# A selective scan whose inputs come back from memory: VectorE's product reads delta B in PSUM

## The chip, the cores and the metric

The kernel runs on one core of a Trainium2 chip. The core has five engines that follow their own queues and meet at semaphores: TensorE (PE in the profile), VectorE (DVE), ScalarE (ACT), GpSimd (POOL), and SyncE (SP), which here only issues DMAs. The metric is the device time of one execution in microseconds (us). Lower is better.

## The reference, cut to what matters

The program is two transformer-like layers over 4 batches of 1024 tokens with 128 channels. The first layer is attention and a mixture of experts; the second is a Mamba-style selective scan and a second mixture of experts. Only the scan is touched by the change:

```python
proj = x_conv @ W_xproj                 # u = x_conv, 128 channels
B_sel, C_sel = proj[..., :16], proj[..., 16:32]
delta = softplus(proj[..., -1])         # one number a token
deltaA = exp(delta[..., None, None] * A)              # A: 128 channels x 16 states
deltaB_u = delta[..., None, None] * B_sel[:, :, None, :] * u[..., None]
def step(h, inp):
    a_t, bu_t, c_t = inp
    h = a_t * h + bu_t                  # 128 x 16 recurrences
    y_t = einsum('bdn,bn->bd', h, c_t)
    return h, y_t
...
y = y + x_conv * D_param
y = y * silu(z)
return y @ W_out
```

Each batch has 128 x 16 = 2048 independent recurrences of 1024 steps.

## The kernel before

The scan stage is one block, `selective_scan`. A tile has 128 partitions (rows) and the 1024 tokens of a batch along the free side. A **group** is 8 channels x 16 states = 128 rows, so a batch has 16 groups and the stage 64. For each group:

- ScalarE makes `da`, the exponential of delta times A (L2098), up to `AHEAD` = 3 groups ahead, into five buffers.
- TensorE makes the group's rows of delta times u, by multiplying with a 0/1 matrix `sel` that copies each of 8 channels to 16 rows. To keep float32 it does this twice, for a rounded part `du_hi` and for the remainder `du_lo` (L1938, L1939: 2 halves of 512 tokens, so 4 matmuls a group). The result lies in one of two PSUM tiles, `ps_x`. Before it writes one, TensorE waits for the scan two groups back.
- VectorE multiplies `ps_x` in place by `brep`, the 16 states' B repeated over the rows (L1995), and runs the recurrence over the tokens as one instruction (L2000), which writes `st`. The scan waits for the product (same engine, by a semaphore), for `da`, and for a free `st` buffer.
- GpSimd multiplies `st` by `crep` into `hc` (L2110).
- Every fourth group TensorE sums `hc` over the states into `ps_y` (L1949).

The order of all this is one list, `scan_plan()`. Every engine walks the same list and does its part of each step, in order, so a step that waits holds everything behind it on its engine. Between the groups of batch b stand the steps that prepare batch b+1: normalisation and transpose (`norm`, `turn`, L2045, L1907, L2049), a causal convolution by four shifted matmuls (`conv`, L1900) and its activation (`u`, L2056), the gate (`z`), the row for delta (`raw`, `soft`, L2069 to L2078), delta itself on VectorE (`delta`, L1976, behind group 9), B and C repeated over the rows (`rep`, TensorE L1919, ScalarE L2089), and `du` and `du_lo`. For the first batch VectorE makes `du` and `du_lo` (L1980, L1983); for the other three GpSimd does (L2116, L2122). In every batch ScalarE makes `du_hi` between them (L2084). Between the groups of batch b also stand the last steps of batch b-1: `y` (L2011), `out` (L1926, L2017) and `stats` (L156, L160). `turn`, `conv`, `z`, `raw`, `rep` and `out` share two PSUM banks, `ps_w`, in turn.

SyncE's whole part in this block is two loads of `sel`, 512 KB each, at its start. VectorE converts them (L1986, L1988).

The two lines that VectorE runs 64 times each are

```python
e.wait_ge(x_pe.sem, x_pe.at[key])                    # TensorE has filled ps_x[i]
e.tensor_tensor(ps_x[i][:, :], ps_x[i][:, :], brep[k][:, :], ALU.mult)        # L1995
...
e.tensor_tensor_scan(st[n % NST_BUF], da[n % NDA], ps_x[i], 0.0, ALU.mult, ALU.add)   # L2000
```

## Time and profile before

| | |
|---|---|
| median of 3 runs | 1983.67 us (1980.42 to 1984.81) |
| the profiled execution | 1981.38 us, of which the recorded span is 1979.6 us |
| the scan's block in the span | from 1370 us to 1661 us, 15% |
| busy over the whole span | PE 82%, POOL 65%, DVE 61%, ACT 39% |
| busy between 1394 and 1646 us | DVE 235.9 of 252 us, POOL 180.2, PE 176.8, ACT 139.2 |
| first and last scan (L2000) | start at 1396.3 and at 1644.9 us |

Read the busy shares stage by stage. The page's shares of the whole span say that TensorE is the busiest engine, and in attention it is. In the scan's block VectorE is, at 94%. The table of stretches, the groups of instructions by line, and the order of instructions in time are the views that show this stage. In a row of the timeline, the number in brackets is the idle time of that engine just before, with what ended it.

### The profile page before, as it was taken

How to read it: one execution, taken by the hardware profiler on the slowest of the kernel's cores; microseconds unless marked ns; L12 is line 12 of the kernel's file. 1: busy time of each engine (PE TensorE's matmuls, PEld its weight loads, DVE VectorE, ACT ScalarE, POOL GpSimd, SP SyncE). 2: the span in 40 equal slices, each digit the busy share in tenths (PEclk: the TensorE clock that was granted, in tenths of full speed). 3: DMA queues.
4: the chain of work that ended last, by engine and by line, in shares of the span. 5: the costliest groups of instructions: out<-in, count | busy, mean ns of one | idle time of the engine just before them, and what ended most of it. 6: DMA issues, size and time to landing. Idle time of an engine off the chain costs nothing. (4 is left out here: it accounts for less than half of the span.)

```text
span 1979.6 us, 26522 instructions
## 1 busy us (share of the span) xinstructions
PE 1617.7 (82%) x9024; PEld 1115.1 (56%) x9024; DVE 1201.4 (61%) x2409; ACT 764.4 (39%) x1278; POOL 1288.5 (65%) x1091
## 2 busy tenths in 40 slices
PE   5799999999999999999999899998776765347670
PEld 3455656665567556676565787886333333236560
DVE  6876666667665666756661456664799997511124
ACT  2245444354443544434445333222866530102120
POOL 4588898789887898878888511100477775481516
PEclk7799999999999999999999999999988876577885
DMA  6223122112211222121210200000000002022213
GB/s 168 65 76 96 44 65 65 37 40 65 54 44 44 65 47 51 41 68 40 58 33 12 62 1 1 1 1 22 0 1 0 0 0 88 29 71 66 79 50 83
DMA packets 82740, 90.67 MB, mean 46 GB/s; under 512 B 12448, under 2 KB 52276, under 8 KB 82608
## 3 DMA queue, kind: packets, MB, share of 16 engines
q1 hardware_dynamic: 78512, 80.97, 16.6%
q0 software_dynamic: 4096, 8.02, 1.4%
q8 instruction: 73, 1.20, 0.3%
q14 instruction: 59, 0.48, 0.1%
HBM read 24.05 MB, written 14.68 MB: 20 GB/s over the span
## 5 line engine op out<-in xcount | busy, mean ns | idle before, releaser
L835 DVE CUSTOM_DVE_ANT_0 ring<-ring,mask 128x128 f32<-128x128 f32 (+7 forms) x512 | 383.8, 769 | 184.3 <-PE ring L697 183.8
L921 ACT ACTIVATE prob<-ring 128x512 f32<-128x512 f32 x576 | 315.2, 597 | 297.0 <-PE ring L712 293.2
L975 POOL TENSOR_TENSOR acc<-acc,prob 128x512 f32<-128x512 f32 x272 | 353.6, 1300 | 72.6 <-ACT prob L921 48.8
L728 PE MATMUL ps_o<-prob,v 128*64 128x256 f32 x2304 | 281.5, 386 | 4.2 <-issue 3.8
L697 PE MATMUL ring<-k,x 128*128 128x512 f32 (+3 forms) x768 | 249.6, 405 | 37.3 <-ACT prob L921 22.3
L711 PE MATMUL ring<-x,k 128*128 128x512 f32 x576 | 257.2, 447 | 25.0 <-DVE neg_m L835 15.7
L712 PE MATMUL ring<-x,k 128*128 128x512 f32 x576 | 229.1, 398 | 0.0
L697 PEld LDWEIGHTS ring<-k,x 128*128 128x128 f32 x768 | 136.4, 197 | 145.1 <-ACT prob L921 51.2
L728 PEld LDWEIGHTS ps_o<-prob,v 128*64 128x64 f32 x2304 | 154.0, 136 | 106.1 <-issue 38.4
L972 POOL TENSOR_TENSOR acc<-prob 128x512 f32<-128x512 f32 x144 | 184.1, 1279 | 7.9 <-ACT prob L921 6.6
L942 POOL TENSOR_TENSOR other<-other,sin 128x512 f32<-128x512 f32 x96 | 136.5, 1422 | 58.1 <-DVE other L814 57.6
L711 PEld LDWEIGHTS ring<-x,k 128*128 128x128 f32 x576 | 109.1, 189 | 99.8 <-issue 43.6
L2000 DVE TENSOR_TENSOR_SCAN m_st<-m_da,m_ps_x 128x1024 f32<-128x1024 f32 x64 | 146.4, 2287 | 2.2
L2310 POOL DMA_INDIRECT c_got<-slots_out,d_slot x64 | 66.1, 1032 | 110.9 <-DMA slots_out<-wo 92.0
L944 POOL TENSOR_TENSOR rot<-rot,other 128x512 f32<-128x512 f32 x96 | 129.7, 1351 | 7.5
L1666 POOL TENSOR_TENSOR first_h<-first_h,e_scaled 128x512 f32<-128x512 f32 x8 | 10.2, 1276 | 175.3 <-DVE e_scaled L1548 175.3
L712 PEld LDWEIGHTS ring<-x,k 128*128 128x128 f32 x576 | 109.6, 190 | 19.6 <-issue 6.9
L2110 POOL TENSOR_TENSOR attn_t<-m_st,m_crep 128x1024 f32<-128x1024 f32 x32 | 78.7, 2459 | 62.1 <-DVE m_st L2000 62.1
L827 DVE TENSOR_TENSOR rot<-rot,other 128x512 fp32r<-128x512 f32 x64 | 72.3, 1130 | 69.6 <-ACT other L903 69.6
L1534 DVE TENSOR_TENSOR e_both<-e_silu,ps_moe 128x512 f32<-128x512 f32 x88 | 60.4, 687 | 87.5 <-PE ps_moe L1378 69.0
L2234 DVE CAST c_xt_hi<-c_tr 128x512 fp32r<-128x512 f32 x16 | 11.1, 692 | 166.0 <-PE c_tr L2189 116.4
L2213 PE MATMUL c_dn<-w,c_hid 128*128 128x128 f32 x512 | 70.3, 292 | 49.9 <-issue 48.8
(302 smaller groups left out, 3179.8 us busy)
## 6 DMA issues: line engine op xcount, KB each, us to landing
x<-other SPq DMA_DIRECT2D x256, 128.0 KB, 2.4
x<-rot SPq DMA_DIRECT2D x128, 128.0 KB, 2.4
slots_in<-zeros SPq DMA_DIRECT2D x2, 2048.0 KB, 8.7
slots_out<-wo SPq DMA_DIRECT2D x16, 256.0 KB
gate<-slots_in SPq DMA_DIRECT2D x11, 256.0 KB
e_w<-in_w SPq DMA_DIRECT2D x3, 704.0 KB, 6.7
x<-shift SPq DMA_DIRECT2D x128, 2.0 KB
first_h<-in_x SPq DMA_DIRECT2D x4, 512.0 KB, 4.9
```

The source lines that it names most:

```text
L697: mm = e.matmul(ps[:, c0:c1], x1[g % 2][:, h, qs], k1[g % 3][:, c0:c1], start=True, stop=True)
L711: e.matmul(banks(step, BANK), k1[g % 3][:, ks], x1[g % 2][:, :, qs], start=True, stop=False)
L712: e.matmul(banks(step, BANK), k2[g % 3][:, ks], x2[g % 2][:, :, qs], start=False, stop=True).then_inc(s2_pe.sem, 1)
L728: mm = e.matmul(ps_o[s * D:(s + 1) * D, qb % 2 * 2 * P:(qb % 2 + 1) * 2 * P], v[g % 2][:, kb, :], prob[i % NPROB][:, s * 2 * P:(s + 1) * 2 ...
L835: e.tensor_tensor_reduce(ps, ps, mask_1[:, SEQ - n:SEQ], 1.0, -3.0 * NEG, ALU.add, ALU.min, neg_m[g % 2][:, c, h, qb % QPC:qb % QPC + 1]). ...
L921: e.activation(prob[i % NPROB][:, :], banks(("s2",) + key, BANK), ACT.Exp, scale=-1.0).then_inc(s2_exp.sem, 1)
L942: e.tensor_tensor(other[i][:, :], other[i][:, :], sin[:, cc], ALU.mult).then_inc(rotated.sem, 1)
L944: e.tensor_tensor(rot[i][:, :], rot[i][:, :], other[i][:, :], ALU.add).then_inc(rotated.sem, 1)
L972: e.tensor_tensor(total[:, :], first[:, :], tile[:, :], ALU.add).then_inc(summed.sem, 1)
L975: e.tensor_tensor(total[:, :], total[:, :], tile[:, :], ALU.add).then_inc(summed.sem, 1)
L2000: e.tensor_tensor_scan(st[n % NST_BUF][:, :], da[n % NDA][:, :], ps_x[i][:, :], 0.0, ALU.mult, ALU.add).then_inc(scan_dve.sem, 1)
L2110: e.tensor_tensor(hc[(b * NG + g) % NHC][:, :], st[r][:, :], crep[b % 2][:, :], ALU.mult).then_inc(hc_pool.sem, 1)
```

## The change

What the change does, in the order of the data:

- The repeated u comes by DMA. When ScalarE has made half of u (512 tokens), SyncE writes it to a new tensor in memory, `u_mem`. For each group SyncE then reads the group's 8 rows back, 16 times over, into a 128-row tile `x_rep`. There are `NX` = 5 such buffers with a semaphore each. The read waits for both halves of u, and for the product five groups back (it has read the buffer).
- TensorE's 256 matmuls by `sel` are gone, with `sel` and its two loads, `du`, `du_hi`, `du_lo`, and the PSUM tiles `ps_x`.
- delta times B is made once a batch and lies in a PSUM tile `ps_b`. For the first batch VectorE makes it (`delta_b`). For the others GpSimd multiplies `brep` by delta in place, and ScalarE copies the result to `ps_b` in a new step `b_in`, which waits for GpSimd and for the last product of the batch before. `brep` now has one buffer where it had two.
- VectorE's product reads `x_rep` in SBUF and `ps_b` in PSUM and writes a PSUM tile `ps_bu`. There is one `ps_bu`, so each product waits for the scan just before it. The first product of a batch also waits for `ps_b`.
- The rows of a tile are ordered by state and then channel (before: by channel and then state). That changes only the layout of `log_a`, `fold`, `w_b` and `w_c`.

```diff
-        steps += [[("rep", b, 0, 0)], [("rep", b, 0, 1), ("delta", b)], [("rep", b, 1, 0), ("du", b)], [("rep", b, 1, 1), ("du_lo", b)]]
+        steps += [[("rep", b, 0, 0)], [("rep", b, 0, 1), ("delta", b)], [("rep", b, 1, 0), ("delta_b", b)], [("rep", b, 1, 1)]]
...
             plan += ahead[g]
+            if g == NG - 1 and b + 1 < BATCH:
+                plan.append(("b_in", b + 1))
...
-                    for c in range(NC2):
-                        cc = slice(c * BANK, (c + 1) * BANK)
-                        e.matmul(ps_x[i][:, cc], sel[:, of * P:(of + 1) * P], du_hi[k][:, cc], start=True, stop=False)
-                        mm = e.matmul(ps_x[i][:, cc], sel[:, of * P:(of + 1) * P], du_lo[k][:, cc], start=False, stop=True)
-                    mm.then_inc(x_pe.sem, 1)
...
                 elif kind == "group":
                     b, g = key
-                    k, i, n = b % 2, (b * NG + g) % 2, b * NG + g
-                    e.wait_ge(x_pe.sem, x_pe.at[key])
+                    n = b * NG + g
+                    e.wait_ge(x_in[n % NX], (n // NX + 1) * 16)
                     if g == 0:
+                        e.wait_ge(*b_ready(b))
                         e.wait_ge(act.sem, act.at["rep", b, 1, NC2 - 1])
-                    e.tensor_tensor(ps_x[i][:, :], ps_x[i][:, :], brep[k][:, :], ALU.mult).then_inc(bu_dve.sem, 1)
+                    if n:
+                        e.wait_ge(scan_dve.sem, scan_dve.at[behind(b, g, 1)])
+                    e.tensor_tensor(ps_bu[:, :], x_rep[n % NX][:, :], ps_b[:, :], ALU.mult).then_inc(bu_dve.sem, 1)
...
-                    e.wait_ge(*du_made("du", b))
-                    if b >= 2:
-                        e.wait_ge(x_pe.sem, x_pe.at[b - 2, NG - 1])
-                    e.activation(du_hi[b % 2][:, :], du[:, :], ACT.Copy).then_inc(act.sem, 1)
+                    e.wait_ge(delta_b_pool.sem, delta_b_pool.at["delta_b", b])
+                    e.wait_ge(bu_dve.sem, bu_dve.at[b - 1, NG - 1])
+                    e.activation(ps_b[:, :], brep[:, :], ACT.Copy).then_inc(act.sem, 1)
...
         def sync(e):
-            e.dma_start(sel_in[:, :], a["sel"][:, 0:half]).then_inc(sel_in0, 16)
-            e.dma_start(y[:, :], a["sel"][:, half:2 * half]).then_inc(sel_in1, 16)
+            for step in plan:
+                kind, key = step[0], step[1:]
+                if kind == "u":
+                    b, c = key
+                    cc = slice(c * BANK, (c + 1) * BANK)
+                    e.wait_ge(act.sem, act.at[step])
+                    e.dma_start(u_mem[b, :, cc], u[b % 2][:, cc]).then_inc(u_out, 16)
+                elif kind == "group":
+
+                    at = key[0] * NG + key[1]
+                    for n in range(at + NX - 1 if at else 0, min(at + NX, BATCH * NG)):
+                        b, g = divmod(n, NG)
+                        rows = slice(group_at(g) * FG, (group_at(g) + 1) * FG)
+                        e.wait_ge(u_out, (b + 1) * NC2 * 16)
+                        if n >= NX:
+                            e.wait_ge(bu_dve.sem, bu_dve.at[behind(b, g, NX)])
+                        e.dma_start(x_rep[n % NX][:, :], u_mem[b, rows, :].rearrange("(o c) t -> o c t", o=1).to_broadcast([NST, FG, SEQ])).then_inc(x_in[n % NX], 16)
```

ScalarE's queue at the start of the scan, from the raw row of delta (`m_raw`) to the first exponentials (`m_da`), before:

```order
L2069 ACTIVATE m_raw<-m_ps_w 128x512 x2
L2074 ACTIVATE m_soft<-m_raw 128x1024
L2078 ACTIVATE m_soft<-m_soft 128x1024
L2089 ACTIVATE m_brep<-m_ps_w 128x512 x2
L2084 ACTIVATE m_du_hi<-m_du 128x1024
L2089 ACTIVATE m_crep<-m_ps_w 128x512 x2
L2098 ACTIVATE m_da<-m_delta,m_a_neg 128x1024 x4
```

and of the changed kernel:

```order
L2054 ACTIVATE m_raw<-m_ps_w 128x512 x2
L2059 ACTIVATE m_soft<-m_raw 128x1024
L2063 ACTIVATE m_soft<-m_soft 128x1024
L2075 ACTIVATE m_brep<-m_ps_w 128x512 x2
L2075 ACTIVATE m_crep<-m_ps_w 128x512 x2
L2084 ACTIVATE m_da<-m_delta,m_a_neg 128x1024 x4
```

The rounding of du, which waited for VectorE, no longer stands between B's rows and C's.

ScalarE's queue where batch 0 ends and batch 1 begins (`m_z` is the gate of batch 0, the three `m_da` behind it are for groups 16 to 18), before:

```order
L2062 ACT_TABLE_LOAD
L2062 ACTIVATE m_z<-m_ps_w 128x512 x2
L2064 ACT_TABLE_LOAD
L2098 ACTIVATE m_da<-m_delta,m_a_neg 128x1024 x3
L2045 ACTIVATE m_xn<-first_h,m_nmr,m_rstd 128x128 x4
```

and of the changed kernel:

```order
L2047 ACTIVATE m_z<-m_ps_w 128x512 x2
L2049 ACT_TABLE_LOAD
L2084 ACTIVATE m_da<-m_delta,m_a_neg 128x1024 x2
L2068 ACTIVATE m_ps_b<-m_brep 128x1024
L2084 ACTIVATE m_da<-m_delta,m_a_neg 128x1024
L2030 ACTIVATE m_xn<-first_h,m_nmr,m_rstd 128x128 x4
```

The copy of delta B to PSUM is put in after the exponential for group 18, and before that for group 19.

SyncE's queue from the start of the block, where before there were the two loads of `sel`, now reads:

```order
L2122 DMA u_mem<-m_u 128x512 x2
L2132 DMA m_x_rep<-u_mem 128x1x1024 x8
L2122 DMA u_mem<-m_u 128x512
L2132 DMA m_x_rep<-u_mem 128x1x1024 x2
L2122 DMA u_mem<-m_u 128x512
L2132 DMA m_x_rep<-u_mem 128x1x1024 x14
```

The two writes of the next batch's u stand among the reads for this batch's groups: the first between the reads for groups 7 and 8, the second between those for 9 and 10.

## Rows read from the trace of the kernel before

**Rows 1.** By stretch: us; busy PE, PEld, DVE, ACT, POOL; clock; DMA share; GB/s.

```profile
1394.00:1460.00 66.00, 45.95 (x165) 23.22 (x166) 56.67 (x34) 48.03 (x58) 41.28 (x18) 0.85 0.00 1
1580.00:1646.00 66.00, 38.03 (x149) 18.55 (x147) 65.13 (x56) 14.98 (x13) 46.73 (x22) 0.76 0.00 0
```

**Rows 2.** DVE groups by line, 1365 to 1652 us: busy, mean ns | idle before, releasers.

```profile
L2000 DVE TENSOR_TENSOR_SCAN m_st<-m_da,m_ps_x 128x1024 f32<-128x1024 f32 x64 | 146.4, 2287 | 2.2
L1995 DVE TENSOR_TENSOR m_ps_x<-m_ps_x,m_brep 128x1024 f32<-128x1024 f32 x64 | 77.6, 1213 | 14.0 <-PE m_ps_x L1939 13.8
```

**Rows 3.** DVE in order of time at the scan's start.

```profile
1388.91 1.23 DVE L1976 SCALAR_TENSOR_TENSOR m_delta<-m_raw,m_soft 128x1024 f32<-128x1024 f32 x1 [12.21 <-ACT m_soft L2078]
1390.17 1.23 DVE L1980 TENSOR_TENSOR m_du<-m_delta,m_u 128x1024 f32<-128x1024 f32 x1
...
1395.08 1.23 DVE L1995 TENSOR_TENSOR m_ps_x<-m_ps_x,m_brep 128x1024 f32<-128x1024 f32 x1 [1.34 <-PE m_ps_x L1939]
1396.34 2.29 DVE L2000 TENSOR_TENSOR_SCAN m_st<-m_da,m_ps_x 128x1024 f32<-128x1024 f32 x1
1402.12 1.23 DVE L1995 TENSOR_TENSOR m_ps_x<-m_ps_x,m_brep 128x1024 f32<-128x1024 f32 x1 [3.49 <-PE m_ps_x L1939]
```

**Rows 4.** DVE in order of time, steady state, and a wait.

```profile
1443.19 2.29 DVE L2000 TENSOR_TENSOR_SCAN m_st<-m_da,m_ps_x 128x1024 f32<-128x1024 f32 x1
1445.40 1.21 DVE L1995 TENSOR_TENSOR m_ps_x<-m_ps_x,m_brep 128x1024 f32<-128x1024 f32 x1
1446.64 2.29 DVE L2000 TENSOR_TENSOR_SCAN m_st<-m_da,m_ps_x 128x1024 f32<-128x1024 f32 x1
1452.58 1.23 DVE L1995 TENSOR_TENSOR m_ps_x<-m_ps_x,m_brep 128x1024 f32<-128x1024 f32 x1 [3.66 <-PE m_ps_x L1939]
```

**Rows 5.** ACT in order of time at the scan's start.

```profile
1382.53 0.69 ACT L2056 ACTIVATE m_u<-m_ps_w,m_cb 128x512 f32<-128x512 f32 x1 [2.75 <-PE m_ps_w L1900]
...
1388.78 1.07 ACT L2089 ACTIVATE m_brep<-m_ps_w 128x512 f32<-128x512 f32 x2
```

**Rows 6.** PE in order of time at the scan's start: C's rows.

```profile
1389.41 1.98 PE L1919 MATMUL m_ps_w<-m_u,m_w_c 128*128 128x512 f32 x4 [2.25 <-ACT m_brep L2089]
```

**Rows 7.** ACT groups by line, 1365 to 1652 us.

```profile
L2089 ACT ACTIVATE m_crep<-m_ps_w 128x512 f32<-128x512 f32 x8 | 4.6, 584 | 0.3 <-PE m_ps_w L1919 0.2
L2084 ACT ACTIVATE m_du_hi<-m_du 128x1024 fp32r<-128x1024 f32 x4 | 4.2, 1057 | 23.0 <-POOL m_du L2116 21.4 <-DVE m_du L1980 1.6
```

**Rows 8.** DMA issues: KB each, median us to landing.

```profile
m_st<-in_sel SPq DMA_DIRECT2D x1, 512.0 KB, 3.8
wo<-in_sel SPq DMA_DIRECT2D x1, 512.0 KB, 5.2
first_h<-in_x SPq DMA_DIRECT2D x4, 512.0 KB, 4.9
first_h<-in_x SPq DMA_DIRECT2D x2, 256.0 KB, 3.2
```

**Rows 9.** PE groups by line, 1365 to 1652 us.

```profile
L1938 PE MATMUL m_ps_x<-m_du_hi,m_sel 128*128 128x512 f32 x128 | 68.2, 533 | 41.4 <-DVE m_st L2000 39.0 <-DVE m_du_lo L1983 2.5
L1939 PE MATMUL m_ps_x<-m_du_lo,m_sel 128*128 128x512 f32 x128 | 56.3, 440 | 0.0
```

**Rows 10.** PE alone by stretch: us, busy (instructions), clock, DMA.

```profile
1446.00:1449.00 3.00, 3.00 (x16) 0.50 0.02 5
```

**Rows 11.** PE in order of time: the state sums, and two taps of the convolution.

```profile
1415.07 1.92 PE L1949 MATMUL m_ps_y<-attn_t,m_fold 128*32 128x512 f32 x16 [1.20 <-POOL attn_t L2110]
1416.93 1.99 PE L1900 MATMUL m_ps_w<-attn_t,m_w_tap 128*128 128x512 f32 x4
...
1445.74 3.64 PE L1949 MATMUL m_ps_y<-attn_t,m_fold 128*32 128x512 f32 x16 [1.51 <-POOL attn_t L2110]
```

**Rows 12.** ACT and POOL in order of time: from a scan to the next batch's delta.

```profile
1412.64 2.38 POOL L2110 TENSOR_TENSOR attn_t<-m_st,m_crep 128x1024 f32<-128x1024 f32 x1 [1.07 <-DVE m_st L2000]
...
1418.95 0.69 ACT L2056 ACTIVATE m_u<-m_ps_w,m_cb 128x512 f32<-128x512 f32 x1 [3.59 <-PE m_ps_w L1900]
...
1430.15 1.06 ACT L2078 ACTIVATE m_soft<-m_soft 128x1024 f32<-128x1024 f32 x1
```

More of the change, by code:

```diff
@@ L1700 @@
 NDA, AHEAD, NST_BUF = 5, 3, 4
+NX, NW = 5, 2
 def group_at(i):
@@ L1723, in scan_plan @@
         plan += [("conv", 0, c, j) for j in reversed(range(TAPS))] + [("u", 0, c)]
-    plan += [("table", 0), ("raw", 0, 0), ("raw", 0, 1), ("soft", 0), ("sel",), ("rep", 0, 0, 0), ("rep", 0, 0, 1), ("delta", 0), ("du", 0),
-             ("du_lo", 0), ("rep", 0, 1, 0), ("rep", 0, 1, 1)]
+    plan += [("table", 0), ("raw", 0, 0), ("raw", 0, 1), ("soft", 0), ("rep", 0, 0, 0), ("rep", 0, 0, 1), ("delta", 0), ("delta_b", 0),
+             ("rep", 0, 1, 0), ("rep", 0, 1, 1)]
     pend = []
```

115 lines of the change are left out of this document (46 added, 69 removed).

## The prediction, made before the changed kernel ran

> **What bounds the kernel now.** The views were read in this order: the table of stretches, VectorE's groups by line, VectorE's instructions in order of time, then the engines that feed it. In the scan's block VectorE is busy 56.7 of 66 us in an early stretch and 65.1 of 66 in the last one, and no other engine comes near [rows 1]. Two lines carry it: 64 scans of 2.287 us and 64 products of 1.213 us, 224 us together [rows 2]. VectorE's idle time before a product sums to 14.0 us, of which 13.8 ended when TensorE had filled `ps_x` [rows 2]. The reader should see three numbers there: the scan and the product are at a fixed duration, the idle time is only 14 us, and all of it is TensorE's. So a change that relieves TensorE can win at most these 13.8 us and what it saves before the first scan. TensorE's own removed work, 68.2 + 56.3 us of matmuls [rows 9], is worth nothing by itself, because VectorE covers it.
>
> **VectorE's two steps themselves don't get shorter.** Before, the product reads one tile in PSUM (`ps_x`) and one in SBUF (`brep`) and writes PSUM. After, it reads `ps_b` in PSUM and `x_rep` in SBUF and writes PSUM. The scan reads `da` in SBUF and a PSUM tile in both. The places are the same in number and kind; only the product is no longer in place. An elementwise step of the same size on SBUF alone (delta, du) takes 1.23 us [rows 3], as the product does behind an idle time. So I take no change of duration. The bound on both sides is 0.02 us each, the difference between a product at 1.21 and one at 1.23 [rows 4]: 64 x 0.02 = 1.3 us.
>
> **The start of the scan: a gain of 3.0 us.** Before, delta starts at 1388.91 and the first product only at 1395.08, because du, its rounding on ScalarE, du_lo and four matmuls stand between [rows 3]. After, delta is followed by one product, `delta_b`, by the 0.03 us after which du follows delta now: 1388.91 + 1.26 + 1.23 = 1391.40. But the first group's product also waits for C's last rows. TensorE makes them from 1389.41 to 1391.39 [rows 6], and ScalarE's copy of the last half takes 0.58 [rows 7], so it ends at about 1392.0. Before, this was hidden behind du_hi. The product starts at 1392.05 and the scan 1.26 later (1395.08 to 1396.34, [rows 3]), at 1393.3. That is 3.0 us before 1396.34. The first exponential takes 1.14 us behind C's rows and ends in time.
>
> **Does the first read of u arrive by then?** u's second half is ready at 1382.53 + 0.69 = 1383.2 [rows 5]. No row shows the landing of a write to memory; the nearest is a 256 KB load, 3.2 us. A 512 KB load with 4 KB rows, as `x_rep` is, lands after 3.8 us [rows 8]. So 1383.2 + 3.2 + 3.8 plus 0.1 for the issue is 1390.3, before 1392.05. The margin is 1.7 us. If the write took 5 us the loss would be 0.1, so I take 0, with 0 to 2 us as the bounds.
>
> **The waits for TensorE: a gain of 12.5 us.** Of the 13.8 us, 1.3 lie before the first product and are counted above. The others (3.49 and 3.66 are the largest, [rows 3, 4]) go, if what replaces TensorE is in time. What is late next? `x_rep` is asked for when the product five groups back has ended, so four groups or some 14 us ahead. The two loads of `sel`, of the same size and shape, landed 3.8 and 5.2 us after issues 0.4 us apart [rows 8], so the second needed 1.8 us more. VectorE uses 512 KB in 3.6 us. `da` is made three groups ahead and loses a wait: ScalarE now idles 21.4 us for GpSimd's du [rows 7]. For `ps_b` ScalarE must copy 1024 columns between the last product of a batch and the next product. A copy of that size takes 1.06 us [rows 7], the scan above it 2.29: hidden, with some 1.1 us to spare. If ScalarE were late by its longest other step of the kind, 1.14 us, it would cost 3 x 0.1. Behind this wait stands only the exponential for group 19, needed three groups later. On SyncE the writes of u hold the reads behind them until ScalarE has made u; the reads for groups 8 and 10 then start some 4 us late, against a lead of 14.
>
> **The new wait for the scan: a loss of 5.5 us.** Now the product starts 2.21 us after the scan's start, and the scan takes 2.29: it starts 0.08 before the scan is recorded as ended [rows 4]. With a wait for an instruction of the same engine, the next starts 0.03 after the end (delta at 1388.91 takes 1.23, du starts at 1390.17) [rows 3]. A product that starts so is also the longer kind, and its scan follows after 1.26 instead of 1.24. A group thus goes from 2.21 + 1.24 = 3.45 to 2.29 + 0.03 + 1.26 = 3.58, or 0.135 us more. Of 63 places between two groups, 18 have other VectorE work between (delta, y, out, stats: 1, 6, 6 and 5 in the four batches), which covers the wait. Another 5 are those where VectorE already idled for TensorE right after a scan; they lose 0.03 each. The other 40 lose 0.135. Together 5.4 + 0.15 = 5.5 us. The bounds are 0 (it costs nothing) and 63 x 0.16 = 10.
>
> The Trainium skill speaks to this place: its page "VectorE: DVE Perf Modes", section "The DRAIN you can't avoid", says that the next instruction can't start before the pipe of the last is empty, and that a semaphore between two instructions costs nothing extra. By that rule the loss would be 0 and the time that of the first rival below. The row shows a start 0.08 us before the recorded end where nothing is waited for and 0.03 after it where something is, so I go by the row.
>
> **The sum.** 3.0 + 12.5 - 5.5 = 10.0 us. The profiled execution took 1981.38, of which the span is 1979.6; 10.0 less is 1971.4. It lies 2.3 below the median of the three runs, so in the terms of the median the forecast is 1983.67 - 10.0 = 1973.7 us. Behind the scan nothing changes: the last sums, y and out wait for GpSimd and run as before.
>
> **Rival 1, the wait is free.** The loss of 5.5 is 0 because the start 0.08 early is only overlap in the record. The time is 1983.7 - 15.5 = 1968.2. For it: the recorded end may lie behind the last read. Against it: the scan behind the product waits too, and starts 1.24 after a product of 1.21. Chance 0.12.
>
> **Rival 2, TensorE's clock drops and the preparation of the next batch becomes late.** From 1446 to 1449 us TensorE is busy throughout at a granted clock of 0.50, the lower of its levels (1.2 of 2.4 GHz) [rows 10]. There the state sums take 3.64 us instead of 1.92, behind an idle time of 1.51 [rows 11]. With 124 us of matmuls gone TensorE will idle more often, and more of the block may run so. The tightest chain in the first batch: a scan ends, GpSimd multiplies (1412.64 to 1415.02), TensorE sums (1.92) and does two taps (1.99), ScalarE makes u at 1418.95 and the last step of softplus at 1430.15 [rows 11, 12]. From the scan's end at 1412.6 that is 18.6 us, and at the lower clock 1.7 + 2.0 more, 22.3. VectorE asks for it six groups later, after 6 x 3.58 = 21.5 us. So it waits 0.8 us, and in the next two batches not at all, since out and stats stand between too. With as much again at `y` in each batch, up to 3 us. The time is 1976.7. Chance 0.14.
>
> **Rival 3, a longer product.** If reading one PSUM tile and writing another costs 0.1 us a product, 6.4 us of the 10 are lost, and at 0.16 all. The time is 1980 to 1986. For it speaks only that no row shows this form. Chance 0.10.
>
> **Rival 4, slower: the reads of u don't keep pace.** Each read fetches the same 8 rows 16 times, and no row shows such a read. VectorE will need 248.6 - 12.5 + 5.5 = 241.6 us from the first scan to the last, 3.83 a group on average. The mechanism decides from there: below 137 GB/s VectorE waits for memory at every group. If each read took the 4.9 us of a 512 KB load in the first stage [rows 8], one after another, 64 of them take 314 us, 69 more than 64 x 3.83. That is 1973.7 + 69 = 2043 us. Against it: the two loads of `sel` ran at 1.8 us each. Chance 0.08. That u isn't in the rows where it is needed, and the change doesn't do what it says, I rule out by the code.
>
> **How the numbers follow.** The forecast has 0.56. A measurement of this kernel can tell about 0.2% (4 us) from no change, so faster means below 1979.7. Forecast and rival 1 and most of rival 2 lie there: 0.56 + 0.12 + 0.12 = 0.80, and I take 0.79. Rival 3 and the rest of rival 2 are the same, 0.12. Slower is rival 4, 0.09 with the odd case. The range takes in rival 1 with 2 us for the spread of the runs (1966) and reaches through rival 2 and half of rival 3 (1983); rival 4 lies outside.
>
> **What would show it.** In the profile after: 64 products at 1.21 to 1.23 us, each starting 0.03 us after its scan's end, a group at 3.58 us; no idle time of VectorE before a product beyond 3 us in all; the first scan 3 us earlier after delta's start (4.4 us behind it where it is 7.4 now); reads of 512 KB landing in under 6 us; PEclk lower in the block. I am wrong if VectorE waits for `x_rep` at more than the first group, if the product's mean is above 1.25, if delta waits for softplus in more than one batch, or if the first product waits for `u_mem`.

## The result, and the profile after

| | before | after | ratio, 95% interval |
|---|---|---|---|
| first comparison, 13 runs each | 1983.42 us | 1978.71 us | 0.9978 [0.9970, 0.9987] |
| once more on another chip, 28 and 6 runs | 1933.61 us | 1927.39 us | 0.9966 [0.9954, 0.9978] |
| span of the profiled execution | 1979.6 us | 1975.8 us | |
| first and last scan | 1396.3 and 1644.9 | 1394.3 and 1639.2 | |

The change makes the kernel faster by 0.2 to 0.3%, some 4.4 to 6.6 us, where 10.0 were forecast. The time lies in the range that was given, but the size was wrong by about a factor of two. The second row is from a chip on which a later stage did less work (last section), so only its ratio is used.

VectorE's groups by line of the kernel after, 1365 to 1652 us, answer to [rows 2]:

```profile
L1985 DVE TENSOR_TENSOR_SCAN m_st<-m_da,m_ps_bu 128x1024 f32<-128x1024 f32 x64 | 146.3, 2286 | 2.2
L1980 DVE TENSOR_TENSOR m_ps_bu<-m_x_rep,m_ps_b 128x1024 f32<-128x1024 f32 x64 | 78.4, 1225 | 5.9 <-ACT m_crep L2075 0.8 <-DVE m_st L1985 0.5
```

The product's idle time has fallen from 14.0 to 5.9 us, and nothing in it is TensorE's any more. The scan is as long as it was, the product 12 ns longer. From this view the block should be some 8 us shorter. It is less, and the next one tells why. VectorE in order of time at the scan's start, the counterpart of [rows 3]:

```profile
1389.80 1.23 DVE L1966 SCALAR_TENSOR_TENSOR m_delta<-m_raw,m_soft 128x1024 f32<-128x1024 f32 x1 [15.09 <-ACT m_soft L2063]
1391.06 1.23 DVE L1970 TENSOR_TENSOR m_ps_b<-m_brep,m_delta 128x1024 f32<-128x1024 f32 x1
1393.06 1.23 DVE L1980 TENSOR_TENSOR m_ps_bu<-m_x_rep,m_ps_b 128x1024 f32<-128x1024 f32 x1 [0.76 <-ACT m_crep L2075]
1394.32 2.29 DVE L1985 TENSOR_TENSOR_SCAN m_st<-m_da,m_ps_bu 128x1024 f32<-128x1024 f32 x1
1396.71 1.23 DVE L1980 TENSOR_TENSOR m_ps_bu<-m_x_rep,m_ps_b 128x1024 f32<-128x1024 f32 x1
1397.98 2.29 DVE L1985 TENSOR_TENSOR_SCAN m_st<-m_da,m_ps_bu 128x1024 f32<-128x1024 f32 x1
```

The first scan starts 4.52 us after delta, where it was 7.43. The two scans here are 3.66 apart, and so are nearly all that have no other work between: of the 63 distances 45 are of this kind, 44 of them 3.65 to 3.68 long and one 4.01. In the kernel before, the plain distance is 3.445. Within a group, the product starts 2.39 after the scan's start (2.21 in [rows 4]) and the next scan 1.265 after the product's (1.24). Of this, idle time shows half, and without a name. The product's 5.9 us are 0.8 and 0.5 that the view puts down to somebody and 4.6 that it doesn't, which is 0.10 at each of these places (a scan of 2.29, the product 2.39 after its start). The other half can't show there: before, the product started 0.08 us ahead of the scan's recorded end, and the loss of such an overlap is no idle time. **Distances from scan to scan** are the view that shows all of it.

Stretches (us; busy PE, PEld, DVE, ACT, POOL; clock; DMA share; GB/s), beside [rows 1]:

```profile
1394.00:1460.00 66.00, 34.55 (x118) 12.12 (x119) 63.67 (x38) 51.31 (x64) 43.47 (x19) 0.77 0.66 164
1580.00:1646.00 66.00, 19.41 (x92) 6.38 (x96) 59.50 (x53) 12.70 (x12) 43.74 (x21) 0.58 0.36 88
```

VectorE is busy 63.7 us of the early stretch (56.7 before). TensorE lost a quarter and half of its work, and its granted clock fell from 0.85 to 0.77 and from 0.76 to 0.58. The DMA engines, idle before, move 164 GB/s. The transfers by issue (KB each, median us to landing) and ScalarE's copy of delta B:

```profile
m_x_rep<-u_mem SPq DMA_DIRECT2D x64, 512.0 KB, 4.6
u_mem<-m_u SPq DMA_DIRECT2D x8, 256.0 KB, 2.0
```

```profile
L2068 ACT ACTIVATE m_ps_b<-m_brep 128x1024 f32<-128x1024 f32 x3 | 3.1, 1021 | 7.6 <-DVE m_ps_bu L1980 7.6
```

The reads land in 4.6 us (median; 11.0 at most), against a lead of four groups, and no product waits for one.

**The ledger of the block.** From distances between scans: the groups in which VectorE waited for TensorE were 13.5 us longer than others of their kind, and all of that is gone. The 45 groups with nothing else between scan and product are 0.21 us longer each, 9.5 us, and the one at 4.01 another 0.35. (What holds that one isn't known. It is the 57th distance in the changed kernel, in its second run, with short reads, with more matmuls, and in the kernel before with the wait added, so neither the reads nor the new tiles make it.) That makes -13.5 + 9.5 + 0.35 = -3.65; the distance from first to last scan went from 248.55 to 244.85, -3.70. With the 2.9 us at the start, the block gives 6.6 us.

### The profile page after: what moved, and what is told of

Read it like the earlier page. It is cut to its first block and busy times, and to the rows that moved or that the text cites. A ratio compares the mean times of both kernels' runs of the same rounds, so it can differ in the third digit from the quotient of the medians.

```text
span 1975.8 us, 26070 instructions
## 1 busy us (share of the span) xinstructions
PE 1554.1 (79%) x8768; PEld 1067.1 (54%) x8768; DVE 1204.6 (61%) x2406; ACT 763.2 (39%) x1277; POOL 1277.5 (65%) x1088
## 5 line engine op out<-in xcount | busy, mean ns | idle before, releaser
L1985 DVE TENSOR_TENSOR_SCAN m_st<-m_da,m_ps_bu 128x1024 f32<-128x1024 f32 x64 | 146.3, 2286 | 2.2
L2096 POOL TENSOR_TENSOR attn_t<-m_st,m_crep 128x1024 f32<-128x1024 f32 x32 | 78.2, 2443 | 59.8 <-DVE m_st L1985 59.8
L960 POOL TENSOR_SCALAR_AFFINE_SELECT prob<-prob 128x512 f32<-128x512 f32 x128 | 91.2, 713 | 24.6 <-ACT prob L921 23.6
```

The costliest lines, as they stand in the source:

```text
L960: e.affine_select(tile[:, :], tile[:, :], [[0, G], [1, P]], ALU.is_ge, 0.0, base=0, channel_multiplier=-1).then_inc(causal.sem, 1)
L1985: e.tensor_tensor_scan(st[n % NST_BUF][:, :], da[n % NDA][:, :], ps_bu[:, :], 0.0, ALU.mult, ALU.add).then_inc(scan_dve.sem, 1)
```

## The experiments

Each kernel is compared with the kernel before, run beside it on the same chip. That took 1982.5 us beside the wait alone and the three kernels with operands elsewhere, 1932.6 beside short reads, more matmuls and the two spread versions of the changed kernel, and 1933.6 beside the rest. A plain group is the distance between two scans with only the product between them, in which no other engine is waited for.

| run | ratio, 95% interval | first to last scan | plain group |
|---|---|---|---|
| before | 1 | 248.6 us | 3.445 us |
| after | 0.9978 [0.9970, 0.9987] | 244.9 | 3.655 |
| after, again | 0.9966 [0.9954, 0.9978] | 244.8 | 3.655 |
| before, with the wait | 1.0042 [1.0025, 1.0059] | 255.3 | 3.66 |
| product in place in SBUF | 1.0258 [1.0241, 1.0275] | 302.6 | |
| delta B in SBUF | 1.0609 [1.0591, 1.0626] | 370.3 | |
| delta B in SBUF, two tiles | 1.0105 [1.0089, 1.0122] | 269.3 | |
| short reads | 0.9969 [0.9956, 0.9983] | 244.8 | 3.655 |
| more matmuls | 1.0046 [1.0030, 1.0062] | 255.9 | 3.655 |
| after, spread | 0.9935 [0.9919, 0.9951] | 238.6 | 3.655 |
| after, spread, C later | 0.9938 [0.9922, 0.9954] | 238.3 | 3.655 |
| before, spread | 0.9984 [0.9975, 0.9993] | 245.3 | 3.445 |
| after, two whole tiles | 0.9999 [0.9990, 1.0009] | 248.5 | 3.445 |
| after, three banks | 1.0001 [0.9992, 1.0011] | 252.5 | 3.505 |

### The wait alone, in the kernel before

```diff
                     e.wait_ge(x_pe.sem, x_pe.at[key])
+                    if n:
+                        e.wait_ge(scan_dve.sem, scan_dve.at[behind(b, g, 1)])
```

> The kernel before with one edit: each product also waits for the scan just before it. TensorE's matmuls, ps_x and everything else stay. My theory is that this wait is dearer than I predicted, 0.21 us a group (the product starts 0.10 us after the scan's recorded end, not 0.03) at the 40 places where nothing else covers it: the time should rise by 6 to 8.5 us, and the steady group go from 3.45 to 3.65 us. By the number of my prediction it rises by 5.5 us and the group is 3.58. The rival, that the missing gain lies in the new tiles or the reads from memory and the wait costs nothing, expects no change, within 1 us.

Measured: 1990.53 us against 1982.48, +8.0 us. VectorE in order of time, and the product's group:

```profile
1445.11 1.23 DVE L1997 TENSOR_TENSOR m_ps_x<-m_ps_x,m_brep 128x1024 f32<-128x1024 f32 x1
1446.37 2.29 DVE L2002 TENSOR_TENSOR_SCAN m_st<-m_da,m_ps_x 128x1024 f32<-128x1024 f32 x1
1448.76 1.23 DVE L1997 TENSOR_TENSOR m_ps_x<-m_ps_x,m_brep 128x1024 f32<-128x1024 f32 x1
1450.03 2.29 DVE L2002 TENSOR_TENSOR_SCAN m_st<-m_da,m_ps_x 128x1024 f32<-128x1024 f32 x1
```

```profile
L1997 DVE TENSOR_TENSOR m_ps_x<-m_ps_x,m_brep 128x1024 f32<-128x1024 f32 x64 | 78.6, 1229 | 16.7 <-PE m_ps_x L1939 12.2 <-DVE m_st L2002 0.5
```

The old kernel with one more wait has the new kernel's group: 2.39 from scan to product, 1.265 from product to scan. The two tiles, the place of delta B and the reads from memory have no part in it. First to last scan grows by 6.8 us in the trace, less than 45 times 0.21, since at a few places VectorE waited for TensorE anyway. The forecast had priced this wait at 5.5 us, the rival at 0. The time excludes the rival (+5.0 to +11.7 us by its interval); the forecast's size is excluded by the group's length, 3.66 and not 3.58.

### Why delta B lies in PSUM: two inputs in SBUF

Three kernels put the operands elsewhere. In the first there is no `ps_bu`: the product overwrites `x_rep`, and the scan reads `da` and `x_rep`, both in SBUF. The wait for the scan is gone (the next read into the buffer waits for the scan instead).

```diff
-                    if n:
-                        e.wait_ge(scan_dve.sem, scan_dve.at[behind(b, g, 1)])
-                    e.tensor_tensor(ps_bu[:, :], x_rep[n % NX][:, :], ps_b[:, :], ALU.mult).then_inc(bu_dve.sem, 1)
+                    e.tensor_tensor(x_rep[n % NX][:, :], x_rep[n % NX][:, :], ps_b[:, :], ALU.mult).then_inc(bu_dve.sem, 1)
...
-                    e.tensor_tensor_scan(st[n % NST_BUF][:, :], da[n % NDA][:, :], ps_bu[:, :], 0.0, ALU.mult, ALU.add).then_inc(scan_dve.sem, 1)
+                    e.tensor_tensor_scan(st[n % NST_BUF][:, :], da[n % NDA][:, :], x_rep[n % NX][:, :], 0.0, ALU.mult, ALU.add).then_inc(scan_dve.sem, 1)
```

> The changed kernel without ps_bu: the product writes back into its x_rep buffer in SBUF and the scan reads it there, so no product waits for a scan (the next read into a buffer waits for the scan instead). The wait theory expects a steady group of 3.45 us and a time 9 us below the changed kernel, near 1969.5 us or 14 us below before. The rival here: the scan now has two inputs in SBUF, beside GpSimd's steady multiplications; if that port is shared, scans or GpSimd's products get longer, by 0.2 us or more each, and the gain is gone.

Measured: 2033.21 us, +51, where the wait theory expected -14. Groups of VectorE and GpSimd:

```profile
L1983 DVE TENSOR_TENSOR_SCAN m_st<-m_da,m_x_rep 128x1024 f32<-128x1024 f32 x64 | 201.7, 3152 | 2.2
L1978 DVE TENSOR_TENSOR m_x_rep<-m_x_rep,m_ps_b 128x1024 f32<-128x1024 f32 x64 | 76.4, 1194 | 1.0 <-ACT m_crep L2073 0.8 <-issue 0.3
L2094 POOL TENSOR_TENSOR attn_t<-m_st,m_crep 128x1024 f32<-128x1024 f32 x32 | 101.6, 3181 | 62.6 <-DVE m_st L1983 62.6
```

The product with one input in SBUF and one in PSUM is fast (1194 ns), and the wait's price is saved. The scan with two inputs in SBUF takes 3152 ns for 2286, and GpSimd's product 3181 for 2443. In order of time the two engines are seen to take turns, the scan ending 2.15 us after GpSimd's step:

```profile
1427.93 2.35 POOL L2094 TENSOR_TENSOR m_hc<-m_st,m_crep 128x1024 f32<-128x1024 f32 x1 [2.23 <-DVE m_st L1983]
1429.00 3.43 DVE L1983 TENSOR_TENSOR_SCAN m_st<-m_da,m_x_rep 128x1024 f32<-128x1024 f32 x1
```

The second kernel leaves the scan as it is and gives the product two inputs in SBUF: delta B stays in two `brep` tiles, and ScalarE's copy goes away.

```diff
-        brep, crep = sb("brep"), [sb(f"crep{i}") for i in range(2)]
+        brep, crep = [sb(f"brep{i}") for i in range(2)], [sb(f"crep{i}") for i in range(2)]
...
-                    e.tensor_tensor(ps_bu[:, :], x_rep[n % NX][:, :], ps_b[:, :], ALU.mult).then_inc(bu_dve.sem, 1)
+                    e.tensor_tensor(ps_bu[:, :], x_rep[n % NX][:, :], brep[b % 2][:, :], ALU.mult).then_inc(bu_dve.sem, 1)
...
-                    e.activation(ps_b[:, :], brep[:, :], ACT.Copy).then_inc(act.sem, 1)
```

> The changed kernel with delta B left in SBUF in two buffers and no copy to PSUM: the product reads two tiles in SBUF and writes the one ps_bu, and waits for the scan as in the changed kernel. Only the place of one input changes. If the place of delta B doesn't matter, the time is the changed kernel's, within 1.5 us, and the product 1.23 us. If two inputs in SBUF beside GpSimd cost, product or GpSimd's step get longer; at 0.2 us a product that is 13 us slower.

Measured: 2102.38 us, +120, nine times the 13 that were named. GpSimd and VectorE in order of time:

```profile
1504.10 2.35 POOL L2089 TENSOR_TENSOR attn_t<-m_st,m_crep 128x1024 f32<-128x1024 f32 x1
1504.13 3.42 DVE L1978 TENSOR_TENSOR m_ps_bu<-m_x_rep,m_brep 128x1024 f32<-128x1024 f32 x1
1507.58 2.29 DVE L1983 TENSOR_TENSOR_SCAN m_st<-m_da,m_ps_bu 128x1024 f32<-128x1024 f32 x1
```

The end of a scan releases both engines at once. GpSimd's step starts 0.03 us earlier and takes its usual 2.35; the product takes 3.42 and ends 1.10 after it, about its own length of 1.2. So it did next to nothing while GpSimd worked. The third kernel uses the two banks (a bank is 512 columns of PSUM) that delta B left free for a second `ps_bu`, so that the product waits for the scan two back (against the changed kernel; the lines of the second kernel are in it too):

```diff
-                    if n:
-                        e.wait_ge(scan_dve.sem, scan_dve.at[behind(b, g, 1)])
-                    e.tensor_tensor(ps_bu[:, :], x_rep[n % NX][:, :], brep[b % 2][:, :], ALU.mult).then_inc(bu_dve.sem, 1)
+                    if n >= 2:
+                        e.wait_ge(scan_dve.sem, scan_dve.at[behind(b, g, 2)])
+                    e.tensor_tensor(ps_bus[n % 2][:, :], x_rep[n % NX][:, :], brep[b % 2][:, :], ALU.mult).then_inc(bu_dve.sem, 1)
...
```

> As the one with delta B in SBUF, and the PSUM room so won holds a second ps_bu: a product waits only for the scan two groups back. Against that kernel only the wait is removed. The wait theory expects a group of 3.45 us and 9 us less than that kernel. The prediction's size expects 5.5 us less; the rival that the wait costs nothing expects no difference.

Measured: 2002.17 us, 100 less than its neighbour and 20 more than the kernel before. Nine less than the neighbour had been expected, so this pair doesn't price the wait: taking it away also moved a clash with GpSimd off VectorE at most groups, as the rows show. Only the plain group, 3.445, is as the theory has it. In order of time:

```profile
1502.59 2.29 DVE L1984 TENSOR_TENSOR_SCAN m_st<-m_da,m_ps_bu 128x1024 f32<-128x1024 f32 x1
1504.79 1.21 DVE L1979 TENSOR_TENSOR m_ps_bu<-m_x_rep,m_brep 128x1024 f32<-128x1024 f32 x1
1504.95 3.23 POOL L2090 TENSOR_TENSOR attn_t<-m_st,m_crep 128x1024 f32<-128x1024 f32 x1 [3.49 <-DVE m_st L1984]
...
1508.15 2.34 POOL L2095 TENSOR_TENSOR m_brep<-m_brep,m_delta 128x1024 f32<-128x1024 f32 x1
1508.24 3.35 DVE L1979 TENSOR_TENSOR m_ps_bu<-m_x_rep,m_brep 128x1024 f32<-128x1024 f32 x1
```

Without the wait the product is 0.16 us ahead of GpSimd's step, and now GpSimd's is the one drawn out (3.23 for 2.35). Where GpSimd happened to be first (1508.15), the product pays again (3.35). Whoever starts first goes through, the other stands. The Trainium skill's page "SBUF — State Buffer", section "SBUF: two separate sides", states this as an exclusive lock between a VectorE instruction with two SBUF inputs and a GpSimd instruction that reads SBUF; all three traces agree, with the times above.

For the change this says what its odd placement is worth. Without delta B in PSUM there is a rival that is 20 or 120 us slower than the kernel before, not 5 us faster. But delta B takes two of the eight banks that the block uses, only one product tile is left, and that makes the wait.

### The reads of u, cut to almost nothing

```diff
+                        some = SEQ if n < NX else 16
-                        e.dma_start(x_rep[n % NX][:, :], u_mem[b, rows, :].rearrange("(o c) t -> o c t", o=1).to_broadcast([NST, FG, SEQ])).then_inc(x_in[n % NX], 16)
+                        e.dma_start(x_rep[n % NX][:, 0:some], u_mem[b, rows, 0:some].rearrange("(o c) t -> o c t", o=1).to_broadcast([NST, FG, some])).then_inc(x_in[n % NX], 16)
```

> The changed kernel, with one part left out: from the sixth group on, each read of the replicated channels brings 16 of the 1024 tokens, so the remaining tokens of the tile are those of an earlier group (the output is not the reference's). The number of transfers and all waits stay; the 32 MB that they moved fall to about 3. Theory (the reads are hidden): product 1225 ns, steady group 3.655 us, time within 2 us of the changed kernel's 1978.7, ratio to the kernel before 0.9978. Rival (the reads cost VectorE or the start of the later stages something): the product falls back to the 1213 ns of the kernel before, -0.8 us over 64, and the time to 1976 or less, ratio 0.996.

Measured: 0.9969 [0.9956, 0.9983], the ratio of the changed kernel (0.9966) within its interval, and the product's row is the same to the nanosecond:

```profile
L1980 DVE TENSOR_TENSOR m_ps_bu<-m_x_rep,m_ps_b 128x1024 f32<-128x1024 f32 x64 | 78.4, 1225 | 6.6 <-ACT m_crep L2075 1.4 <-DVE m_st L1985 0.5
```

First to last scan is 244.83 us with short reads and 244.83 with full ones. The 32 MB of reads cost VectorE nothing. The 12 ns by which the product grew are not memory's either: the kernel before with the wait has 1229.

### More matmuls, for TensorE's clock

```diff
+EXTRA = 2
...
+                    if plan.index(step) > plan.index(("group", 0, 0)):
+                        for _ in range(EXTRA):
+                            e.matmul(bank[:, :], w_in[:, HID:2 * HID], h_t[:, cols(0, 0)], start=True, stop=True)
```

> The changed kernel with two further matmuls of 128x512 on TensorE ahead of each matrix product of the preparation from the first group on, into the same bank, whose results are overwritten: some 90 of them at about 0.6 us give back the 55 to 60 us of TensorE's busy time that the change took from the scan block. Theory (the clock in the block is of no account to VectorE): granted clock of the stretch 1400 to 1650 up from 0.72 towards the 0.83 of before, steady group still 3.655, time within 2 us of 1978.7. Rival (the lower clock costs the stages behind the block 1.9 us, since from the last scatter into the experts' slots to the end of the span the changed kernel took 188.2 us and the kernel before 186.1): that stretch falls back to 186.1 us and the time to 1976.8.

Measured: 1.0046, 9 us slower than the kernel before and some 14 slower than the changed one. Both expectations of the time were wrong. As expected, the plain group stayed at 3.655 while the granted clock of the stretch rose from 0.72 to 0.83, so the group's length doesn't come from the clock. But the extra work made the preparation late. VectorE's steps with a wait ahead:

```profile
1429.38 2.30 DVE L1970 SCALAR_TENSOR_TENSOR m_delta<-m_raw,m_soft 128x1024 f32<-128x1024 f32 x1 [1.24 <-ACT m_soft L2067]
...
1456.31 1.23 DVE L1984 TENSOR_TENSOR m_ps_bu<-m_x_rep,m_ps_b 128x1024 f32<-128x1024 f32 x1 [2.89 <-ACT m_ps_b L2072]
...
1473.60 0.69 DVE L2006 TENSOR_TENSOR m_scaled<-m_ps_w,gate 128x512 f32<-128x512 f32 x1 [1.68 <-PE m_ps_w L1933]
...
1479.65 0.69 DVE L2006 TENSOR_TENSOR m_scaled<-m_ps_w,gate 128x512 f32<-128x512 f32 x1 [1.89 <-PE m_ps_w L1933]
```

As a test of what the clock does to the time it fails, since two things changed. It does show how near the preparation stands to VectorE: about 60 us more of TensorE's work, spread over a block where it has over 100 idle, lengthened the block by 11 us. The chain of rival 2 was real, but the clock alone was not enough to pull it.

### The small work spread over the waits

The statistics of four tiles, eight instructions in one place, become one `bn_stats` behind each of four scans and four `bn_aggr` behind a fifth; y's second half comes one group later. Nothing is added or left out.

```diff
+ONE_ROW, FOUR = (5, 6, 7, 8, 11, 12, 13, 14), (10, 15)
...
-            if b and g in (5, 6):
-                plan.append(("stats", b - 1, g - 5))
+            if b and g in ONE_ROW:
+                plan.append(("row", b - 1, *divmod(ONE_ROW.index(g), 4)))
+            if b and g in FOUR:
+                plan.append(("four", b - 1, FOUR.index(g)))
+            if b and g == 2:
+                plan.append(("y", b - 1, 1))
```

> The changed kernel with VectorE's small work spread out, nothing added: the statistics of four tokens' tiles, until now eight instructions in one place, become one instruction behind each of four scans and four behind a fifth, and the second half of y is taken one group later. So 44 of the 63 places between a scan and the product that waits for it hold other work, where 18 did. Theory (the wait costs only where nothing lies between: scan's start to product's start 2.39 us without, 2.20 us and the work itself with work between): 26 x 0.18 = -4.7 us, less some 0.5 us for instructions that no longer follow on each other: the last scan 4.2 us nearer to the first than the 244.85 of the changed kernel, time 1974.5, ratio 0.9956. Rival (the loss lies in the single tile and the product's reads, not in the wait): within 1 us of 1978.7.

Measured: 0.9935 [0.9919, 0.9951], 12.7 us faster than the kernel before; first to last scan 238.6, 6.3 less than after, where 4.2 were expected. VectorE in order of time:

```profile
1477.82 2.29 DVE L1992 TENSOR_TENSOR_SCAN m_st<-m_da,m_ps_bu 128x1024 f32<-128x1024 f32 x1
1480.03 0.27 DVE L2020 BATCH_NORM_STATS2 stats<-first_h 128x6 f32<-128x128 f32 x1
1480.21 1.23 DVE L1987 TENSOR_TENSOR m_ps_bu<-m_x_rep,m_ps_b 128x1024 f32<-128x1024 f32 x1
1481.48 2.29 DVE L1992 TENSOR_TENSOR_SCAN m_st<-m_da,m_ps_bu 128x1024 f32<-128x1024 f32 x1
```

The statistic starts 2.21 us after the scan's start, as the product did in [rows 4], and the product at 2.39, as if nothing stood between. The group is 3.66 with the statistic and 3.655 without. A piece of work of 0.19 us is free in the shadow of the wait, 24 times. The control is the same spreading in the kernel before, where no product waits for a scan:

> The kernel before with the same spreading of the statistics and of y's halves as in the spread version, and nothing else. Theory (the spreading pays only where a product waits for the scan ahead of it, because a statistic of 0.2 us then stands in time that was idle anyway): in the kernel before no product waits for a scan, each single statistic adds its 0.19 us to a group of 3.45, the distance from first to last scan stays at 248.5 us within 1, ratio 1.000. Rival (spreading saves for a reason of its own, such as the wait between statistics and aggregates): -6 us as in the changed kernel, ratio 0.997.

Measured: 0.9984 [0.9975, 0.9993], first to last scan 245.3, so 3.3 less where 0 was expected. The same place in this kernel:

```profile
1487.86 2.29 DVE L2007 TENSOR_TENSOR_SCAN m_st<-m_da,m_ps_x 128x1024 f32<-128x1024 f32 x1
1490.07 0.27 DVE L2035 BATCH_NORM_STATS2 stats<-first_h 128x6 f32<-128x128 f32 x1
1490.25 1.22 DVE L2002 TENSOR_TENSOR m_ps_x<-m_ps_x,m_brep 128x1024 f32<-128x1024 f32 x1
1491.50 2.29 DVE L2007 TENSOR_TENSOR_SCAN m_st<-m_da,m_ps_x 128x1024 f32<-128x1024 f32 x1
```

Here the group is 3.64 with a statistic and 3.445 without: the 0.19 us are paid. That is the core of the theory. But spreading has a gain of its own that I had not foreseen, and the distances divide it. Some 2.2 us lie where VectorE waits for TensorE: 5.47 and 4.73 us at two places became 4.57 and 4.58, and at 5.80 and 5.39 a statistic was added and the distances are 5.02 and 5.39. Another 1.1 us are the statistics themselves: in one place the eight instructions make a group 1.18 us longer, apart 4 x 0.19 + 0.27 = 1.03, and the last four `bn_aggr` now fall behind the last scan. Only this second part can be in the changed kernel too, which has no waits for TensorE. Without it, its gain is 6.3 - 1.1 = 5.2, and that is what the theory gives: 44 places with other work, where there were 18, are 26 more, at some 0.2 us each.

In a further version the rows of C come behind the first group's exponentials, and GpSimd's first step waits for them in the product's stead (the first line is VectorE's, the others GpSimd's):

```diff
-                        e.wait_ge(act.sem, act.at["rep", b, 1, NC2 - 1])
...
+                    if g == 0:
+                        e.wait_ge(act.sem, act.at["rep", b, 1, NC2 - 1])
```

> As the spread version, and at the start of the scan block the rows of C come behind the first group's exponentials: the first product no longer waits for them (it had waited 0.76 us), GpSimd's first step waits in its place. Theory: first scan 4.52 - 0.76 = 3.76 us after the start of delta, 0.8 us less than the spread version; GpSimd's first step begins about 1.5 us later and has 3.65 - 2.37 = 1.3 us a group to make it up; time 1973.7, ratio 0.9952. Rival (GpSimd's late start is handed on by its sums, or the first product waits next for the replicated channels, whose margin was 1.7 us against the first scan): no change to the spread version, or slower.

Measured: 0.9938 [0.9922, 0.9954]. Its start in order of time:

```profile
1388.96 1.23 DVE L1974 SCALAR_TENSOR_TENSOR m_delta<-m_raw,m_soft 128x1024 f32<-128x1024 f32 x1 [15.04 <-ACT m_soft L2082]
1390.22 1.23 DVE L1978 TENSOR_TENSOR m_ps_b<-m_brep,m_delta 128x1024 f32<-128x1024 f32 x1
1391.55 1.23 DVE L1987 TENSOR_TENSOR m_ps_bu<-m_x_rep,m_ps_b 128x1024 f32<-128x1024 f32 x1
1392.82 2.29 DVE L1992 TENSOR_TENSOR_SCAN m_st<-m_da,m_ps_bu 128x1024 f32<-128x1024 f32 x1
```

The first scan comes 3.86 us after delta (4.52 before this step; 3.76 expected), and the last 238.3 after the first, so the trace has 0.7 of the 0.8 us. The times can't tell them from nothing (1921.0 against 1919.9 us). Both spread versions beat the kernel before and the changed one.

### Can the wait be had away and delta B left in PSUM?

Two ways to find the banks. In the first, which leaves out part of the computation (both halves of y are summed into one bank), there are two whole product tiles, and the preparation has one bank for two:

```diff
-        ps_w = [pb(f"ps_w{i}", [P, BANK]) for i in range(NW)]
...
-        ps_b, ps_bu = pb("ps_b", [P, SEQ]), pb("ps_bu", [P, SEQ])
+        ps_w = pb("ps_w", [P, BANK])
+        ps_b = pb("ps_b", [P, SEQ])
+        ps_bu = pb("ps_bu", [P, 4 * BANK])
+        bu = [ps_bu[:, i * SEQ:(i + 1) * SEQ] for i in range(2)]
...
-                    if n:
-                        e.wait_ge(scan_dve.sem, scan_dve.at[behind(b, g, 1)])
-                    e.tensor_tensor(ps_bu[:, :], x_rep[n % NX][:, :], ps_b[:, :], ALU.mult).then_inc(bu_dve.sem, 1)
+                    if n >= 2:
+                        e.wait_ge(scan_dve.sem, scan_dve.at[behind(b, g, 2)])
+                    e.tensor_tensor(bu[n % 2], x_rep[n % NX][:, :], ps_b[:, :], ALU.mult).then_inc(bu_dve.sem, 1)
```

> The changed kernel with two whole tiles in PSUM for the product, so that it waits for the scan two back and no longer for the one just done, while delta B stays in PSUM. The four banks come from elsewhere: the two halves of y are summed into one bank (so y is the sum of both halves and the output not the reference's), and the preparation has one bank from the first group on, with the second output step one group later. Theory (the wait is the whole price of the single tile): steady group 3.45 us with the product at 1213 ns, as in the kernel before; first to last scan 244.85 - 8.9 = 236 us; ratio 0.9978 - 0.0045 = 0.993. Rival (the group is longer because the product reads two operands from other places than before, wait or no wait): steady group stays above 3.6 and the ratio at 0.998.

Measured: 0.9999, first to last scan 248.5. The plain group and two of the new waits:

```profile
1487.14 2.29 DVE L1994 TENSOR_TENSOR_SCAN m_st<-m_da,m_ps_bu 128x1024 f32<-128x1024 f32 x1
...
1493.96 1.21 DVE L1989 TENSOR_TENSOR m_ps_bu<-m_x_rep,m_ps_b 128x1024 f32<-128x1024 f32 x1
1495.20 2.29 DVE L1994 TENSOR_TENSOR_SCAN m_st<-m_da,m_ps_bu 128x1024 f32<-128x1024 f32 x1
```

```profile
1432.87 1.23 DVE L1975 SCALAR_TENSOR_TENSOR m_delta<-m_raw,m_soft 128x1024 f32<-128x1024 f32 x1 [6.50 <-ACT m_soft L2072]
...
1457.00 1.23 DVE L1989 TENSOR_TENSOR m_ps_bu<-m_x_rep,m_ps_b 128x1024 f32<-128x1024 f32 x1 [2.23 <-ACT m_ps_b L2077]
```

The plain group is 3.445 and its product 1.21 to 1.22, at all 47 places without a wait for another engine, with delta B in PSUM and u from memory. So the whole 0.21 us is the wait, and nothing of it the new operands. The time was missed for another reason: 236 us were expected from first to last scan, and the preparation with one bank added 13.3 (6.6 at delta in the first batch, 2.3 at `ps_b`, 4.4 at three output steps), which makes 249. The second way computes everything: one bank more, and the product in halves of 512 columns, the first of which goes to the free bank and waits only for the scan two back:

```diff
+                    for c in (n % 2, 1 - n % 2):
+                        cc = slice(c * BANK, (c + 1) * BANK)
+                        past = behind(b, g, 2 if c == n % 2 else 1)
+                        if past:
+                            e.wait_ge(scan_dve.sem, scan_dve.at[past])
+                        e.tensor_tensor(bu[n % 2][:, cc], x_rep[n % NX][:, cc], ps_b[:, cc], ALU.mult).then_inc(bu_dve.sem, 1)
```

> The changed kernel with a third bank for the product, taken from the preparation (one bank from the first group on, the second output step one group later): products are made in two halves of 512 columns, the half that goes to the free bank first and with no wait for the scan ahead, the other behind it. All is computed. Theory (a half of 0.67 us covers the wait as the small work does): first half 2.20 us after the scan's start, second 0.60 us later, scan 0.70 us after that, so a group of 3.50 for 3.655, but 0.05 more where the wait was covered already: 45 x -0.15 + 18 x 0.05 = -5.9 us, ratio 0.995. Rival (two instructions of 0.67 for one of 1.23 eat up what the wait gives back): -1 to +5 us, ratio 0.9975 to 1.000.

Measured: 1.0001, first to last scan 252.5. In order of time:

```profile
1467.64 1.26 DVE L1991 TENSOR_TENSOR m_ps_bu<-m_x_rep,m_ps_b 128x512 f32<-128x512 f32 x2
1468.94 2.29 DVE L1996 TENSOR_TENSOR_SCAN m_st<-m_da,m_ps_bu 128x1024 f32<-128x1024 f32 x1
...
1481.22 0.69 DVE L2013 TENSOR_TENSOR m_scaled<-m_ps_w,gate 128x512 f32<-128x512 f32 x1 [2.40 <-PE m_ps_w L1937]
```

The group is 3.505, as expected (3.50): halving costs 0.06 and gives 0.21 back. The time was missed (5.9 us less was expected than the changed kernel's, and it is some 6 more), since the same preparation with one bank took 14 us. A bank is worth more there than at the product. A kernel with one product tile and no wait at all was not tried: nothing would then keep the product from overwriting what the scan still reads.

### The changed kernel once more

> The changed kernel once more, unaltered, beside the three that follow. Both readings of the first comparison of the traces expect a ratio to the kernel before of 0.9978. They differ on where the trace's 6.6 us inside the scan block went, of which 4.4 us show in the time: if the rest is chance of a single profile, the ratio lies nearer 0.9967 (-6.6 us) and the stretch from the last scatter to the end is as long in both; if a later stage gives 2 us back, the ratio stays at 0.9978 and that stretch is some 2 us longer than in the kernels whose TensorE does more in the block (139.0 and 138.6 us in the two spread versions on the second chip, 139.1 with the extra matmuls).

Measured: 0.9966 [0.9954, 0.9978], -6.6 us, as the trace's block says. The stretch from the last scatter into the experts' slots to the end is 138.0 us here, and 137.4 (short reads), 139.1 (more matmuls), 139.0 and 138.6 (spread), 137.2 (before, spread), 137.4 and 138.7 (two tiles, three banks) beside it. On the chips of the first runs it was 186.1 (before), 188.2 (after), 186.0, 187.1, 186.7 and 188.9. These scatter by 2 to 3 us and don't follow TensorE's work in the block: with more matmuls it is 139.1. But the shortest on each kind of chip are those of the kernels made from the one before (186.1 and 186.0; 137.2), if only by 0.2 to 0.6 us to the next. The block's 6.6 us lie just outside the interval of the first comparison (2.6 to 6.0 us) and inside that of the second (4.3 to 8.9). So no stage is shown that gives 2 us back, and a loss of 1 to 2 us behind the block isn't excluded.

## Why the prediction was off

**What bounds the block** was right. VectorE carries it before and after; the other engines' losses and gains don't show.

**The durations** were right: scan 2286 for 2287 ns, product 1225 for 1213, 0.8 us over 64 and inside the bound of 1.3. Rival 3 had no part.

**The start** was right: 3.0 us forecast, 2.9 measured. The first product waited for C's rows, as worked out (0.76 us), and the reads were there.

**TensorE's waits** were right: all of the 12.5 us of idle time went, and nothing came in its place. By the distances between scans they were worth 13.5: a product that waits 0.41 us makes its group 0.53 longer, and two groups of 3.70 and 4.73 us were late by 0.25 and 0.15 without a wait in the view.

**The new wait** is the step that failed. The forecast took 0.03 us behind the recorded end, from delta and du in [rows 3], and so a group of 3.58. The product starts 0.10 behind the recorded end of a scan, and the group is 3.655. The price is 0.21 and not 0.135: 40 x 0.075 = 3.0 us. At the 5 places where TensorE had been waited for, the forecast took 0.03 where the traces have 0.10 (the idle 3.49 us went, and 7.05 became 3.66), 0.4 us; one group of 4.01 adds 0.35, and the start 0.1. Against that stand 0.5 us of TensorE's waits that the idle view had not shown. Together that is the 3.4 us between -10.0 and -6.6 in the block. The row that was taken as the nearest is one where a 1.23 us elementwise step lies ahead. The scan is another instruction, and the trace of before had no row in which something waits right behind it except with idle time for TensorE on top. The bound of 0.16 for a place was too low as well. That 9.8 us stayed under the bound of 10 is luck, since it was counted over all 63 places and only 45 lose.

The rule of the Trainium skill's page "VectorE: DVE Perf Modes", section "The DRAIN you can't avoid", that a semaphore between two instructions costs nothing extra (measured there on chains of `tensor_copy`), doesn't hold here: rival 1 has the time that follows from it, and the wait alone costs +8.0 us.

**Rival 2**, the clock: it fell as foretold, from 0.85 to 0.77 in the early stretch, and cost VectorE nothing; delta waited for softplus only at the start. **Rival 4**, slow reads: 64 reads with a median of 4.6 us took nothing: the first five were under way together, and after them one was asked for per group.

## What to carry to other kernels

A wait on the engine's own last instruction costs on VectorE even when it is met at once: here 0.21 us behind a scan, so a single buffer between two steps of one engine has a price, of which idle time shows half and names nobody for it. Look at the distances between like instructions, and put small independent work into such places, where 0.19 us of it is free. Before a buffer is doubled with banks from elsewhere, see what the giver's chain needs: here one bank was worth 13 to 14 us to the preparation, and at the product one bank some 6 and two 9.

## What the runs showed of the hardware that I had not expected

- The wait's price: start to start 2.21 us from a scan to what follows unheld, 2.39 to what waits for it; and 1.24 against 1.265 from the product to the scan behind it.
- A VectorE instruction with two SBUF inputs against GpSimd's product of two SBUF tiles: 1.21 us became 3.42 when GpSimd was 0.03 us ahead, and GpSimd's 2.35 became 3.23 when VectorE was 0.16 ahead. With one of the inputs in PSUM neither moved (changed kernel: scan 2286 ns, product 1225, GpSimd's 2443).
- Eight rows of 4 KB read from memory sixteen times each land in 4.6 us (median), at 164 GB/s in the early stretch, and VectorE's instructions are not a nanosecond longer for it. A 256 KB write landed in 2.0 us, not the 3.2 taken from a load.
- On two of the chips every kernel was some 50 us faster, all of it behind the last scatter into the experts' slots, where TensorE ran some 490 instructions and not some 660 (137 to 139 us, not 186 to 189). What makes that stage do less there stays open.
